# Feed-forward of a macaron block: gates spread through device memory instead of TensorE, gate product first, router a chunk further ahead

## The reference, cut to what matters

```
x = x + 0.5 * ffn(layernorm(x))
x = x + attention(layernorm(x))
x = x + 0.5 * ffn(layernorm(x))

def ffn(x):                                   # 8 experts, 2 of them per row, and a shared one
    scores = softmax(x @ router_w)
    _, sel = top_k(scores + expert_bias, 2)
    gate = where(expert in sel, scores, 0)    # this kernel's form of the top-2 weights
    y = (silu(x @ sw1) * (x @ sw3)) @ sw2
    for e in range(8):
        y += gate[:, e] * ((silu(x @ w1[e]) * (x @ w3[e])) @ w2[e])
    return y
```

## Time and profile before

| | us |
|---|---|
| median of 3 runs | 1351.88 |
| lowest and highest | 1349.77, 1361.17 |
| the profiled execution | 1349.75 |
| its span, first to last instruction | 1348.0 |

### The profile page before, as it was taken

One profiled execution on the slowest core, in us unless ns is written; L12 is line 12 of the kernel. 1 busy time (PEld: TensorE's weight loads), 2 busy tenths in 40 slices (PEclk: granted clock), 3 DMA queues, 4 the chain that ended last, 5 costly groups with the idle time before them and its releaser, 6 DMA issues. The chain is left out here.

```text
span 1348.0 us, 34907 instructions
## 1 busy us (share of the span) xinstructions
PE 1238.0 (92%) x11940; PEld 691.8 (51%) x11940; DVE 1107.1 (82%) x2686; ACT 833.5 (62%) x1477; POOL 554.5 (41%) x658
## 2 busy tenths in 40 slices
PE   5999999999979999999999999899899999999998
PEld 2555555555533555555555555555455555555554
DVE  6888888888975688888888888888688898988876
ACT  5665565656543566666666666666565656566564
POOL 3454544544530233333333333333354554554444
PEclk9999999999995799999999999999899999999999
DMA  6000000000000000000000000000000000000000
GB/s 186 2 1 1 0 0 0 0 0 0 1 1 1 1 1 2 2 2 2 2 2 2 1 2 2 1 2 2 2 2 16 9 16 8 16 8 16 8 9 25
DMA packets 21417, 11.85 MB, mean 9 GB/s; under 512 B 960, under 2 KB 21312, under 8 KB 21312
## 3 DMA queue, kind: packets, MB, share of 16 engines
q1 hardware_dynamic: 21312, 10.43, 2.8%
HBM read 6.23 MB, written 4.19 MB: 8 GB/s over the span
## 5 line engine op out<-in xcount | busy, mean ns | idle before, releaser
L672 POOL TENSOR_TENSOR h_lo<-h,h_hi 128x512 f16<-128x512 f32 x288 | 337.7, 1173 | 386.3 <-ACT h_hi L634 375.6
L1109 DVE TENSOR_REDUCE neg_max_at<-score_at 128x2 f16<-128x512 f32 (+1 forms) x384 | 254.4, 692 | 78.1 <-PE score_at L940 72.5
L1229 POOL TENSOR_SCALAR_AFFINE_SELECT probs_at<-probs_at 128x512 f32<-128x512 f32 x256 | 157.0, 637 | 352.4 <-ACT probs_at L1187 351.9
L634 ACT ACTIVATE h_hi<-h 128x512 f16<-128x512 f32 x288 | 180.6, 627 | 152.7 <-DVE h L435 150.8
L1187 ACT ACTIVATE probs_at<-prob_at 128x512 f32<-128x512 f32 x384 | 201.6, 598 | 79.3 <-PE prob_at L972 77.4
L435 DVE TENSOR_TENSOR h<-prod,gate_b 128x512 f32<-128x512 f32 x256 | 174.9, 683 | 53.9 <-PE gate_b L543 53.7
L564 PE MATMUL y_b<-w_hi,h_hi 128*128 128x128 f16 x1152 | 207.8, 219 | 2.6 <-POOL h_lo L672 2.6
L564 PE MATMUL y_b<-w_hi,h_lo 128*128 128x128 f16 x1152 | 207.8, 219 | 0.0
L564 PE MATMUL y_b<-w_lo,h_hi 128*128 128x128 f16 x1152 | 207.8, 219 | 0.0
L429 DVE TENSOR_TENSOR prod<-silu,b 128x512 f32<-128x512 f32 x256 | 175.5, 686 | 37.9 <-ACT silu L623 23.6
L623 ACT ACTIVATE silu<-a 128x512 f32<-128x512 f32 x288 | 169.7, 589 | 49.7 <-PE a L530 48.3
(11 more groups left out here) (138 smaller groups left out, 2203.4 us busy)
## 6 DMA issues: line engine op xcount, KB each, us to landing
x<-in_L_attn_x_dram SPq DMA_DIRECT2D x16, 256.0 KB, 3.0
out_dram<-x SPq DMA_DIRECT2D x16, 256.0 KB, 2.3
raw_w<-in_L_ffn_w_dram SPq DMA_DIRECT2D x3, 512.0 KB, 5.2
raw_w<-in_L_ffn_sw_dram SPq DMA_DIRECT2D x3, 64.0 KB, 4.1
raw_attn<-in_L_attn_W_Q_dram SPq DMA_DIRECT2D x1, 64.0 KB, 4.9
raw_attn<-in_L_attn_W_K_dram SPq DMA_DIRECT2D x1, 64.0 KB, 3.6
raw_attn<-in_L_attn_W_V_dram SPq DMA_DIRECT2D x1, 64.0 KB, 3.6
raw_attn<-in_L_attn_W_O_dram SPq DMA_DIRECT2D x1, 64.0 KB, 3.7
```

The lines of the kernel that those rows point to most:

```text
L634: nc.scalar.activation(h_hi[k][:, :], h[k][:, :], ACT.Copy).then_inc(hhi_done, 1)
L672: nc.gpsimd.tensor_tensor(h_lo[k][:, :], h[k][:, :], h_hi[k][:, :], ALU.subtract).then_inc(hlo_done, 1)
L1109: nc.vector.tensor_reduce(dst, src, AX.X, ALU.max, negate=True).then_inc(max_done, 1)
L1229: nc.gpsimd.affine_select(out=p, in_=p, compare_op=ALU.is_ge, fill=0.0, base=0, pattern=[[0, GROUPS], [1, P]], channel_multiplier=-1).then ...
```

## The change

The gates no longer pass through TensorE and a bank. `turn_gates` turns them in float32 with one transpose, ScalarE copies the result to `gate_rows` (32 partitions x 128), SyncE stores it to device memory (`spread_gates`), waits for that, and loads it back eight times, once per expert, each load repeating one row of 2 KB on all 128 partitions (`gate_wide`, two sets). VectorE now makes prod = b * gate_wide first and then h = prod * silu; silu is written by ScalarE over a in PSUM (step 0: to `silu_shared`). So the a bank is held until h is done, not only until silu is. The bank of the gates becomes `turn_bank`, in which x and the gates are turned. The router runs two chunks ahead (x in three buffers), the gates one chunk ahead, and most intermediate tensors of the gates lie in `r_bank` (PSUM). The gates have 19 steps, not 21. The order of a chunk is new: `norm` after step 0, `scale` after step 2, `residual` after step 3, `split_x` after step 4 on VectorE; `expd` in step 0 on ScalarE; `norm_root` after step 0 on GpSimd. The loop over pairs of chunks is written out in full. Cut to its core:

```diff
-GATE_PLACES = (0, 0, 0, 0, 0, 0, 0, 2, 2, 4, 5, 7, 7, 9, 10, 12, 13, 15, 16)
-GATE_STEPS = 21
+GATE_STEPS = 19
+GATE_PLACES = (2, 2, 2, 4, 6, 8, 10, 12, 14, 16) + (GATE_STEPS,) * (2 * STEPS - 9)
+GATE_PLACES_FIRST = (0, 0) + (GATE_STEPS,) * (2 * STEPS - 1)
+GATES_BEGIN = (7, 1)
+X_AHEAD = 6
...
+        for i, n in enumerate(("logits", "expd", "score", "biased", "hit", "rank", "rest", "second")):
+            g[n] = r_bank[:, i * TILES * EXPERTS:(i + 1) * TILES * EXPERTS].rearrange("p (t e) -> p t e", e=EXPERTS)
...
+            def spread_gates(c):                       # SyncE
+                sp.wait_ge(rows_done, c + 1)
+                wait_count(sp, prod_done, (c - 1) * EXPERTS)
+                sp.dma_start(gates_dram[c % 2], gate_rows[:, :]).then_inc(rows_stored, DMA)
+                sp.wait_ge(rows_stored, (c + 1) * DMA)
+                for e in range(EXPERTS):
+                    wait_count(sp, gate_loaded[e], c * DMA)
+                    row = gates_dram[c % 2][e * TILES:(e + 1) * TILES, :].rearrange("(a t) n -> a (t n)", a=1)
+                    sp.dma_start(gate_wide[c % 2][:, e, :], row.to_broadcast([P, CHUNK])).then_inc(gate_loaded[e], DMA)
...
             def swiglu(c, e):                          # VectorE
-                nc.vector.tensor_tensor(prod[:, :], silu[k][:, :], b_bank[k][:, :], ALU.mult).then_inc(prod_done, 1)
+                wait_count(dve, h_done, n - 1)
+                dve.wait_ge(gate_loaded[e - 1], (c + 1) * DMA)
+                nc.vector.tensor_tensor(prod[k][:, :], b_bank[k][:, :], gate_wide[c % 2][:, e - 1, :],
+                                        ALU.mult).then_inc(prod_done, 1)
                 beside(c, e, 0)
-                dve.wait_ge(gate_b_done, gated + 1)
-                nc.vector.tensor_tensor(h[e % 3][:, :], prod[:, :], gate_bank[:, :], ALU.mult).then_inc(h_done, 1)
+                dve.wait_ge(prod_done, gated + 1)
+                dve.wait_ge(silu_done, n + 1)
+                nc.vector.tensor_tensor(h[e % 3][:, :], prod[k][:, :], a_bank[k][:, :], ALU.mult).then_inc(h_done, 1)
...
+            def wait_a_free(n):                        # TensorE, before the a matmuls of step n
+                wait_count(pe, silu_done if (n - 2) % STEPS == 0 else h_done, n - 1)
...
-                    if name == "w1" and e > 1:
-                        spread_gate(c, slot, e - 1)
...
             def chunk(c):                              # TensorE
                 for e in range(STEPS):
                     up(c, e)
+                    if c == 0 and e == 1:
+                        turn_gates(0)
+                        router(1)
+                    if e == 4 and c + 2 < CHUNKS + more:
+                        turn_x(c + 2)
+                    if e == (2 if c == 0 else 6) and c + 1 < CHUNKS:
+                        turn_gates(c + 1)
+                    if e == 6 and c + 2 < CHUNKS:
+                        router(c + 2)
...
             def silu_a(c, e):                          # ScalarE
-                nc.scalar.activation(silu[k][:, :], a_bank[k][:, :], ACT.Silu).then_inc(silu_done, 1)
+                dst = silu_shared if e == 0 else a_bank[k]
+                nc.scalar.activation(dst[:, :], a_bank[k][:, :], ACT.Silu).then_inc(silu_done, 1)
...
             def chunk(c):                              # ScalarE
                 for e in range(STEPS):
                     silu_a(c, e)
+                    if c > 0 and e == 0 and c + 1 < CHUNKS:
+                        expd(c + 1)
+                    if e == 4 and c + 2 < CHUNKS + more:
+                        split_x(c + 2)
+                    if e == (2 if c == 0 else 6) and c + 1 < CHUNKS:
+                        take_gates(c + 1)
                     if e > 0:
                         split_h(c, e - 1)
+                    elif c > 0:
+                        split_h(c - 1, STEPS - 1)
...
             def chunk(c):                              # VectorE
                 for e in range(STEPS):
                     swiglu(c, e)
+                    if e == 0 and c + 2 < CHUNKS + 2 * more:
+                        norm(c + 2)
+                    if e == 2 and c + 2 < CHUNKS + 2 * more:
                         scale(c + 2)
+                    if e == 3 and c > 0:
+                        residual(c - 1)
+                    if e == 4 and c + 2 < CHUNKS + more:
+                        split_x(c + 2)
                     beside(c, e, 1)
...
             def chunk(c):                              # GpSimd
                 for e in range(STEPS):
                     low_part(c, e)
-                    if e == 1 and exists(c + 2 - 2 * more):
+                    if e == 0 and c + 2 < CHUNKS + 2 * more:
                         norm_root(pool, nc, norm0 + c + 2, buf, ln_step, ln_rooted)
```

More of the change, by code:

```diff
@@ L256, in ffn_phase, with turned @@
         more = 1 if out is None else 0
-        silu = [sb(f"silu{s}", [P, CHUNK], F32) for s in range(2)]
-        prod = sb("prod", [P, CHUNK], F32)
+        def turned(c):
+            return (c + 2 * (1 - made)) % 3
+        xt_hi, xt_lo = norms["xt_hi"], norms["xt_lo"]
+        silu_shared = sb("silu_shared", [P, CHUNK], F32)
+        prod = [sb(f"prod{s}", [P, CHUNK], F32) for s in range(2)]
         h = [sb(f"h{s}", [P, CHUNK], F32) for s in range(3)]
@@ L262, in ffn_phase @@
         h_lo = [sb(f"h_lo{s}", [P, CHUNK], F16) for s in range(3)]
-        gate_t = [sb(f"gate_t{s}", [2 * EXPERTS, CHUNK], F16) for s in range(2)]
-        g = {n: sb(n, [P, TILES, EXPERTS], F32) for n in
-             ("shifted", "expd", "score", "biased", "hit", "rank", "first", "rest", "second", "gate")}
+        gate_wide = [sb(f"gate_wide{s}", [P, EXPERTS, CHUNK], F32) for s in range(2)]
+        gate_rows = sb("gate_rows", [EXPERTS * TILES, P], F32)
+        g = {n: sb(n, [P, TILES, EXPERTS], F32) for n in ("shifted", "first", "chosen")}
@@ L293, in _, with load_x @@
         def _(sp):
-            if x_dram is not None:
[L295 to L302, removed]
-            if out is not None:
[L304 to L309, removed]
+            def load_x(c):
+                src = x_dram.rearrange("(c p) d -> p c d", p=P)
+                wait_count(sp, x_loaded[c % 2], c // 2 * DMA)
+                sp.dma_start(x[:, c * TILES:(c + 1) * TILES, :],
+                             src[:, c * TILES:(c + 1) * TILES, :]).then_inc(x_loaded[c % 2], DMA)
@@ new lines, in store @@
+            def store(c):
+                dst = out.rearrange("(c p) d -> p c d", p=P)
+                sp.wait_ge(x_added, c + 1)
+                sp.dma_start(dst[:, c * TILES:(c + 1) * TILES, :],
+                             x[:, c * TILES:(c + 1) * TILES, :]).then_inc(stored, DMA)
+            if x_dram is not None:
+                load_x(0)
+                prepare.load(sp)
+                for c in range(1, X_AHEAD):
+                    load_x(c)
+            for c in range(CHUNKS):
+                spread_gates(c)
+                if x_dram is not None and c + X_AHEAD < CHUNKS:
+                    load_x(c + X_AHEAD)
+                if out is not None and c > 1:
+                    store(c - 2)
@@ L408, in gates @@
                     done.then_inc(gate_step, 1)
             def beside(c, e, place):
[L412 to L417 removed]
+                at = GATE_PLACES_FIRST if c == 0 else GATE_PLACES
+                if c + 1 < CHUNKS:
+                    gates(c + 1, at[2 * e + place], at[2 * e + place + 1])
@@ L461, in _ @@
             if not made:
-                norm(0, 0)
+                norm(0)
                 scale(0)
@@ L658, in _ @@
             expd(0)
+            split_x(1)
             if prepare:
                 prepare.high(act, "attn", y_bank[1])
-            run_pairs(act, chunk)
-            split_h(CHUNKS - 1, 1, STEPS - 1)
+            for c in range(CHUNKS):
+                chunk(c)
+            split_h(CHUNKS - 1, STEPS - 1)
         @block.gpsimd
@@ L688, in _ @@
                 norm_root(pool, nc, 1, buf, ln_step, ln_rooted)
-            run_pairs(pool, chunk)
+            for c in range(CHUNKS):
+                chunk(c)
 def select_heads(nc, consts, done):
```

339 lines of the change are left out of this document (146 added, 193 removed).

## The result

The changed kernel takes 1318.32 us (median of 4, 1311.71 to 1322.61) against 1352.31 for the kernel before beside it: a ratio of 0.973 (95% interval 0.967 to 0.980), 34 us less. 1310 was forecast. The profiled execution, 1311.71 us with a span of 1308.9, is the fastest of the four; against the profiled execution of before it gains 38.0.

A forecast was written before the change was run, and what follows sets the result against it. TensorE was taken to set the pace, held twice by the gates, with VectorE a close second. 1349.75 - 36.5 (steady chunks) - 13.8 (last chunks) + 10 (starts) = 1309.5, predicted as 1310 us; range for 8 in 10: 1250 to 1345.

The forecast's parts named there:

- The walk: One chunk followed from the start of a(0) through all engines' queues: 22.0 us, 1.35 less than before.
- The collision: VectorE's `scale` after step 2 meets GpSimd's h_lo(1) and h_lo(2): done at 11.2 us instead of 9.5.
- the rival without it: `scale` gets in before h_lo or waits once only: chunk 20.3 us, time 1264, chance 0.26.
- TensorE's own work: Per chunk, 23.35 less 3.36 for gate spreads and 1.19 at the gates' turn: 18.8 us.
- the rival by TensorE alone: TensorE alone sets the pace, silu, norm and gates all hide: 27 x 4.55, time 1223, chance 0.05.
- PSUM is not dear: Opposite rival: gate steps in PSUM take 0.25 instead of 0.19 us, 1.0 us per chunk, time 1337, chance 0.12.
- The rule of the Trainium skill on access from PSUM: Fixed part 120 cycles against 58: some 65 ns more per gate step, sum some 27 us higher.
- already in the walk: Gate steps in PSUM no longer stretch when h_lo runs; each was taken at 0.21 us.
- The loads were hidden: First expert's gates there 1 us into the next chunk, needed at 3.5; rival that loads set the pace, chance 0.10.
- the steady chunk's gain of 1.35 us: 27 chunks, 1 to 14 of phase 0 and 1 to 13 of phase 1, gain 36.5 us in all.
- The starts: Start of each phase, where chunk 0 waits for its gates: 5 us charged per phase, 10 in all.
- the 4.6 each that was forecast: The three last chunks come near TensorE's floor and gain about 4.6 us each, 13.8 in all.

The follow-up runs named there:

- Experiments 1 and 2: Each against the changed kernel: 1, GpSimd does `norm_root` ahead of a chunk's first h_lo, 1260.78 us; 2, h_lo computed for 16 of 512 columns only, 1263.06 us.
- experiment 3: Silu in place of Exp in `expd`, against the changed kernel: 1258.87 us (one run); its odd chunk, where `scale` met no h_lo, took 19.46 us instead of 20.19.
- The fifth group of experiments: Each against the changed kernel: gate tensors but the logits back in on-chip memory, 1354.07 us; silu back in on-chip memory, 1321.14 us (one run each).

## Why the prediction was right, point by point

**The walk held.** From a(0), forecast and measured: silu(1) 4.84 and 4.82; h(1) 5.48 and 5.49; a(3) 6.2 and 6.23; the root done 8.4 and 8.42; `scale` done 11.2 and 11.24; prod(3) 11.5 and 11.49; a(5) 13.15 and 13.24; the chunk 22.0 and 22.20. The missing 0.2 us come in a(5) to a(7), which starts at 18.26 instead of 18.05.

**The collision is shown as the cause of most of the difference.** Experiments 1 and 2 take it away in two ways, and the chunk falls to 20.11; the rival without it was priced at 20.3 and 1264 us, the two kernels take 1260.8 and 1263.1. The match is not quite the rival's own: 0.49 of the 2.09 us are the wait for the root, which the rival had left in place. The odd chunk of experiment 3 has the same root with and without the collision, and there the 0.73 us by which `scale` ends earlier are the 0.73 by which the chunk is shorter. The Trainium skill (SBUF — State Buffer, Who interferes with whom) says that VectorE and GpSimd share one pair of ports to on-chip memory, and that where a VectorE instruction needs this pair, for two inputs from that memory or in a mode that uses two ports, whichever engine issues first makes the other wait for the whole instruction. The trace agrees in both directions: xn 716 ns beside h_lo and 342 alone, and an h_lo of 1.30 us instead of 1.16 behind an xn.

**TensorE's own work** was put at 18.8 us per chunk; with the other waits nearly removed (0.3 us of a is left) the chunk is 18.98 and the time 1230, where the rival by TensorE alone said 1223.

**PSUM is not dear.** Gate steps of 185 to 200 ns bear out the value that was taken, nothing. The rule of the Trainium skill on access from PSUM (VectorE: DVE Perf Modes, the section on the TRN2 errata), by which 27 us were to be added, does not show here. But the sentence that cost gate tensors in PSUM at nothing mentioned their good side only as "already in the walk". The fifth group of experiments shows what that is worth: with the gate tensors in on-chip memory the kernel takes 1354 us (one run), so without this part the change gains nothing. The walk's 0.21 for a gate step holds only with it.

**The loads were hidden**, with the room shown by doubling them. The issues of the changed kernel show a landing of 5.4 us (columns: count, KB, median us to landing), where 3.0 were taken; below it, the eight loads of one chunk.

```profile
gate_wide<-gate_rows SPq DMA_DIRECT2D x256, 256.0 KB, 5.4
...
DMA to landing us min/median/max: 3.2/5.8/7.1
```

The median is of loads that run eight together, and the first of them, for which the 3.0 us were taken, landed in 3.2. The store before it took 1.4 us, not 2.3. So the first expert's gates, loaded from 1105.25 on, were there at 1108.45, 0.1 us into the next chunk where 1 was forecast; the spare was larger than the forecast had it, and in the steady chunks no prod waits for a load.

**The terms of the sum.** The term that was furthest off is the steady chunk's gain of 1.35 us. In phase 1 the twelve intervals of the earlier trace rows fell from 280.22 to 267.62 us, 1.05 each; in phase 0 thirteen fell from 304.58 to 288.60, 1.23 each. 0.2 us a chunk are the walk's 22.0 for 22.20; in phase 1 two of the twelve took 22.44 and 23.18 us, the longer one with a granted clock of 0.93 where the others have 1.00. 14 x 1.23 + 13 x 1.05 is 30.9, where 36.5 was forecast. The starts were forecast at 5 us each. The first gate step of phase 1 and the next a, on VectorE's and TensorE's timelines:

```profile
946.96 0.19 DVE L345 TENSOR_REDUCE peak<-r_b 128x4 f32<-128x32 f32 x1 [0.82 <-PE r_b L488]
958.85 0.69 DVE L408 TENSOR_TENSOR prod<-b,gate_wide 128x512 f32<-128x512 f32 x1 [0.55 <-DMA gate_wide<-gate_rows]
...
960.32 0.61 PE L523 MATMUL a<-xt_hi,w_hi 128*128 128x512 f16 x1 [1.57 <-DVE h L418]
975.16 0.38 PE L523 MATMUL a<-xt_hi,w_hi 128*128 128x512 f16 x1
```

a(3) comes 13.4 us after the first gate step instead of 7.3, and the a(0) of chunk 1 28.2 instead of 22.1 (990.73 on TensorE's timeline of before): 6 us, where 5 was charged. In phase 0 it is 6 as well: 46.33 instead of 40.29. TensorE came back at the lower clock, as the forecast allowed for: 0.62 granted from 957 to 962 us, 0.70 to 967, then full. What is left of phase 1 is its last two chunks: -17.47 - 6.06 + 13 x 1.05 = -9.9, about the 4.6 each that was forecast. So the steady chunks gave 5.6 us less and the starts took about 2 more than the sum had them: the feed-forwards gained 33.0 us (15.48 and 17.47) where 40.3 were forecast. The profiled execution came within 2.2 us of its forecast, 1309.5, only by a term that was not in the sum: the attention, 6.15 us shorter. That is luck, as the last section shows; the median of 1318.32, 8 us above the forecast, tells the miss better.

## What to carry to other kernels

Before an engine's work is moved a step, look at what GpSimd has in its queue at that moment: here, a short VectorE instruction that waited for GpSimd started just when GpSimd went on to its next long one, and they met in every chunk. A small operation on which another engine waits belongs ahead of the long one in an in-order queue, and at the place where that queue is idle. When one wait is gone, look at TensorE's idle groups again before the next edit: taking the Exp's tables away moved TensorE's wait to the turn of the gates, and ending the gate steps earlier moved it back to a.

## What was not expected of the hardware

The attention, whose code and place in the order are the same, was 6 us shorter. The windows behind the last `residual` of phase 0, of before and then of after (us, TensorE busy with count, granted clock, DMA share, GB/s):

```profile
395.30:425.30 30.00, 20.85 (x91) 0.62 0.00 1
425.30:457.30 32.00, 30.34 (x197) 0.50 0.00 1
```

```profile
379.80:409.80 30.00, 21.39 (x91) 0.53 0.00 1
409.80:441.80 32.00, 28.75 (x273) 0.80 0.00 1
```

In the first 30 us of both TensorE does the same 91 matmuls and the clock falls to the level of 1.2 GHz; before, it stayed there for all of the next 32 us, after the change for about 40% of them (0.80 lies 60% of the way from 0.50 to 1.00), and more matmuls fit in. In the kernel with the root first the second window has 0.77.

The change need not have done this. The code of the attention is the same in all thirteen kernels, and in their profiled executions this stretch took 565.07 us (silu in on-chip memory, granted clock 0.97 over the stretch) to 581.57 us (hardly any h_lo, 0.93); six of the others lie within 1 us of the 573.35 of before. So 6 us lie inside what one execution differs from another. When the clock rises, and why, was not tested.

Eight broadcast loads of 256 KB in a chunk of 22.2 us took 34% of the DMA engines' time, sixteen 61%, and nothing waited for them: a trip of the gates through device memory costs this kernel nothing but its two starts.
